# Loading the softmax divisors into 128 partitions: eight row broadcasts against one load with a repeated dimension

## The chip, the core and the metric

The kernel runs on one core of a Trainium2 chip. Its engines are TensorE (PE, matrix products), VectorE (DVE), ScalarE (ACT), GpSimd (POOL) and SyncE (SP), which here only issues transfers. SP's transfers run on the core's 16 DMA engines. The metric is the device time of one execution in microseconds, lower is better. Times shown are medians of runs of the same program.

## The reference

The reference is a gated cross-attention block followed by a mixture-of-experts block, over x of 4 batches x 1024 rows x 256. Cut to what matters here:

```
kh, vh = heads(ctx @ Wk.T), heads(ctx @ Wv.T)       # 154 keys, 16 heads of 16
qh     = heads(layernorm(x) @ Wq.T) / 4             # 1024 queries
scores = qh . kh + relative bias, causal mask
attn   = softmax(scores)                            # divides by the sum over the keys
x      = x + tanh(g_xattn) * (attn @ vh) @ Wo.T
x      = x + tanh(g_ffn)   * moe(layernorm(x))      # 8 routed experts, top 4, and a shared one
```

The change concerns the division in the softmax: the kernel first forms the products with the unnormalised exponentials, together with their sum over the keys, and then multiplies the products by the reciprocal of that sum.

## The kernel before

**Units.** The attention part works in eight units, numbered u = 2b + h: batch b of four, half h of its 1024 queries (512 queries). On every engine a unit is the function `unit(b, h, carry, ahead)`, with 20 steps `i` on PE, DVE and ACT. Step by step, PE computes the scores of the unit (`sT`, L917 to L924), ACT takes their exponential (`ex`, L503), PE multiplies by the values (`oT`, L938 and L942) and ACT copies the result to `raw` or `raw_first` (L493). Each engine does other work between: for the unit that follows, PE forms the scores again only to find each row's maximum (`smax`, L877), DVE reduces them (`mx`, L604), and PE, ACT and DVE project queries and keys of a later unit (`work`; L811, L822, L853; `ql` on DVE, L572). The maxima go through PE and DVE into `mt` (L659), and a transfer repeats them into `qs` (`qs<-mt`, L278), without which the next unit's scores can't start.

**Divisors.** The sums of a unit stand in four partitions of `raw`. They are divided one unit later. `divisors(u, h)` on SP is a chain of transfers, each of which waits for the one before it: `den_d<-raw` (L286) stores the 4 rows of 2048 sums in DRAM, `dent<-den_d` (L288) brings them back in 128 partitions x 64, DVE takes the reciprocal (L665), `rden_d<-dent` (L292) stores them in DRAM as 4 rows of 2048, and `at<-rden_d` (L296) brings them into the 128 partitions of `at`, in each of which 1024 numbers (4 KB) are wanted. Partition 32 j + 16 k + i needs the half k of row j, the same for all 16 values of i. Four short transfers (L290) shift part of `raw` between. `divide` on DVE (L671) then multiplies in two pieces, at steps 13 and 14 where h = 0 and at 12 and 13 where h = 1. PE projects `at` by `wo` (L953) at the end of the unit, or, for the last two units, in the expert part.

**The order around it.** All orders are written out by hand: each engine's program is a fixed list, and semaphores hold it back. In program order SP issues, after the `at` load: in units with h = 1 the keys of the next batch (`ks<-km`, L271), then queries; in units 2 and 4 (h = 0) only queries (`qs<-qh`, L267), which wait for `ql` of DVE. In unit 6, the last with h = 0, the weights of the expert part follow at once (L1127 and L1129, `cst`, `bias`, `gw` and nine pieces of `wx`), and behind them `qs<-mt`. On DVE, behind the first piece of `divide` in units 2 and 4, stand `ql` and further maxima. In the h = 1 units POOL subtracts the maxima from a whole score tile (L408) at the time at which DVE divides.

The divisors of units 0 to 5 are thus loaded and used in units 1 to 6, those of unit 6 in unit 7 and the first steps of the expert part, those of unit 7 in the expert part. There are eight `divisors` in all.

Of the kernel before, what the change touches and what calls it, by code (L numbers as in the profile page):

```python
# [23 lines left out]
H, HD = 16, 16  # L24
# [4 lines left out]
HALF = 512  # L29
# [53 lines left out]
def attention(nc, outer, ctx, x1, tg, t):  # L83
# [13 lines left out]
    def sb(name, shape, dt=F32, where=ctx):  # L97
        return where.enter_context(nc.sbuf_tensor(name, shape, dt))

    def sem(name):  # L100
        return outer.enter_context(nc.semaphore(name))
# [10 lines left out]
    at = sb("at", [P, 2, HALF], where=outer)  # L112
# [38 lines left out]
    rden_d = nc.dram_tensor("rden_d", (4, NG * HALF), F32).ap()  # L151
# [27 lines left out]
    shift_in, den_out, den_in, rden_s, rden_out, rden_in = sem("shift_in"), sem("den_out"), sem("den_in"), sem("rden"), sem("rden_out"), sem("rden_in")  # L179
# [44 lines left out]
    def batches(eng, unit):  # L224
        body(unit, 0, first=True)
        with eng.Fori(0, B - 2) as k:
            body(unit, k + 1)
        body(unit, B - 1, last=True)
# [18 lines left out]
    def sync(sp, load_weights):  # L247
        for dst, src in ((cst[:], t["cst"][:, 0:NKEPT]), (raw[:, 1, 0:2 * P], t["cst"][:, NKEPT:NKEPT + 2 * P])):
            sp.dma_start(dst, src).then_inc(w_in, 16)
        sp.dma_start(x1[:, 0:TU, :], t["x"][0][:, 0:TU, :]).then_inc(x_first, 16)  # L250
        for dst, src in ((raw[:, 0, :], t["wq"].rearrange("p c d -> p (c d)")), (rel[:], t["rel"]), (gates[:], t["gates"])):
            sp.dma_start(dst, src).then_inc(w_in, 16)
        sp.dma_start(ctxb[:], t["ctx"][0]).then_inc(c_in, 16)
        sp.dma_start(wk[:], t["wk"]).then_inc(kv_in, 16)
        sp.dma_start(wv[:], t["wv"]).then_inc(kv_in, 16)
        sp.dma_start(x1[:, TU:NT, :], t["x"][0][:, TU:NT, :]).then_inc(x_in[0], 16)
        sp.dma_start(wo[:], t["wo"]).then_inc(kv_in, 16)
        sp.wait_ge(kv_in, 3 * 16)
        for i in range(1, B):
            sp.dma_start(x1[:, i * NT:(i + 1) * NT, :], t["x"][i]).then_inc(x_in[i], 16)  # L260

        def q_stack(h, part):

            n = slice(h * HALF, (h + 1) * HALF)
            for r, src in enumerate((qh, ql, qh)):
                for i in (2 * part, 2 * part + 1):
                    sp.dma_start(qs[32 * r:32 * r + 32, i::4, n].bitcast(F32),  # L267
                                 src[32 * i:32 * i + 32, :, :].bitcast(F32)).then_inc(qs_in[h][part], 16)

        def k_stack(g):  # L270
            sp.dma_start(ks[0:96, 2 * g:2 * g + 2, :].bitcast(F32), km[:, 2 * g:2 * g + 2, 0:PAIR].bitcast(F32))\  # L271
                .then_inc(ks_in[g], 16)

        def m_stack(b, h):

            q0 = HALF // 2 if h == 0 else 0
            sp.wait_ge(mT_s, 2 * b + h + 1)
            sp.dma_start(qs[96:128, :, h * HALF + q0:(h + 1) * HALF].bitcast(F32),  # L278
                         mt[:, q0:HALF].unsqueeze(1).broadcast_to([32, NSTK, HALF - q0]).bitcast(F32)).then_inc(ms_in, 16)

        def divisors(u, h):

            kept = raws[h]

            sp.wait_ge(raw_s, NG * (u + 1))
            sp.dma_start(den_d.rearrange("j (g n) -> j g n", g=NG), kept[HD::32, :, :]).then_inc(den_out, 16)  # L286
            sp.wait_ge(den_out, 16 * (u + 1))
            sp.dma_start(dent[:], den_d.rearrange("j (p n) -> (j p) n", p=32)).then_inc(den_in, 16)  # L288
            for j in range(4):
                sp.dma_start(kept[32 * j + HD:32 * j + 32, 0:2, :], kept[32 * j:32 * j + HD, 2:4, :]).then_inc(shift_in, 16)  # L290
            sp.wait_ge(rden_s, u + 1)
            sp.dma_start(rden_d.rearrange("j (p n) -> (j p) n", p=32), dent[:]).then_inc(rden_out, 16)  # L292
            sp.wait_ge(rden_out, 16 * (u + 1))
            for j in range(4):
                for k in range(2):
                    sp.dma_start(at[32 * j + HD * k:32 * j + HD * (k + 1), :, :].rearrange("p g n -> p (g n)"),  # L296
                                 rden_d[j:j + 1, 2 * k * HALF:2 * (k + 1) * HALF].broadcast_to([HD, 2 * HALF]))\
                        .then_inc(rden_in, 16)

        def unit(b, h, carry, ahead):  # L300
            u = 2 * b + h
            if h == 0 and ahead:
                sp.wait_ge(v_ps, b + 1)
                sp.nop().then_inc(waited, 1)
                sp.dma_start(ctxb[:], t["ctx"][b + 1]).then_inc(c_in, 16)
            if carry and (h == 0 or ahead):
                sp.wait_ge(st_ps, NI * u)
                q_stack(1 - h, 1)
            if carry:
                divisors(u - 1, 1 - h)  # L310
            if h == 1 and ahead:
                sp.wait_ge(kl_s, 2 * (b + 2))
                sp.nop().then_inc(waited, 1)
                for g in range(NG - 1):
                    sp.wait_ge(st_ps, NI * u + 5 * (g + 1))
                    k_stack(g)
            if ahead:
                sp.wait_ge(work_free, NW0 + NWORK * b + Q_USE[h] + 2)
                sp.nop().then_inc(waited, 1)
                sp.wait_ge(st_ps, NI * u + 15)  # L320
                q_stack(h, 0)
            if h == 0 and not ahead:
                for part in range(2):
                    sp.wait_ge(qs_in[1][part], 16 * 6 * B)
                load_weights()
            if h == 0:
                m_stack(b, 1)
            elif ahead:
                m_stack(b + 1, 0)
                sp.wait_ge(st_ps, NI * (u + 1))  # L330
                k_stack(NG - 1)

        sp.wait_ge(work_free, 4)
        for part in range(2):
            q_stack(0, part)
        sp.wait_ge(kl_s, 2)
        for g in range(NG):
            k_stack(g)
        sp.wait_ge(work_free, 12)
        for part in range(2):  # L340
            q_stack(1, part)
        m_stack(0, 0)
        batches(sp, unit)
        divisors(2 * B - 1, 1)

    def gpsimd(pool):
# [192 lines left out]
    def vector(dve):  # L539
# [125 lines left out]
            nc.vector.reciprocal(dent[:], dent[:]).then_inc(rden_s, 1)  # L665

        def divide(u, h, groups=range(2)):
            dve.wait_ge(rden_in, 128 * (u + 1))
            dve.wait_ge(shift_in, 64 * (u + 1))
            for g in groups:  # L670
                nc.vector.tensor_tensor(at[:, g, :], raws[h][:, g, :], at[:, g, :], ALU.mult).then_inc(at_s, 1)  # L671
# [14 lines left out]
        def unit(b, h, carry, ahead):  # L686
# [3 lines left out]
            for i in range(NI):  # L690
# [16 lines left out]
                if i in DIVIDE[h] and carry and (h == 0 or ahead):  # L707
                    divide(u - 1, 1 - h, (DIVIDE[h].index(i),))
# [73 lines left out]
        def second_half():  # L782
            unused(Y_USE[0], B, 0)
            for pr in range(2):
                residual(B - 1, 1, pr, NW0 + Y_USE[0] + pr)

        return lambda: divide(2 * B - 2, 0), first_half, lambda: divide(2 * B - 1, 1), second_half

    def tensor(pe):
# [768 lines left out]
```

## Time and profile before

| | |
|---|---|
| median of 3 runs | 726.85 us (726.72 to 727.78) |
| the profiled execution | 730.77 us |
| its span, first to last instruction | 728.7 us |
| PE busy | 619.2 us, 85% of the span |
| DVE busy | 458.8 us, 63% |
| ACT busy | 276.1 us, 38% |
| POOL busy | 178.3 us, 24% |
| packets of SP's queue q1 | 39824, 58.25 MB, 28.9% of 16 DMA engines' span |
| mean granted TensorE clock | 0.938 |

The profiled execution took 730.77 us, of which 728.7 us lie between the first and the last instruction; all times of rows are within this span. A row of the timeline gives the start, the duration, the engine, the line of the kernel and what is written from what; "x8" means eight of one kind in a row, and a bracket tells how long the engine had stood idle and who ended that. "SPq" rows are transfers being issued: their duration is the time to issue, not to land. A row "DMA" in the chain of waits is a transfer in flight, from the start of its issue to its landing.

### The profile page before, as it was taken

The page shows a single profiled execution, that of the slowest core. Times are in us where ns is not written, and L with a number is a line of the kernel's source. Part 1 is how long each engine was busy: PE and PEld are TensorE (multiplying, and loading weights), DVE is VectorE, ACT ScalarE, POOL GpSimd, SP SyncE. Part 2 cuts the span into 40 slices and gives each one's busy share as a digit, 9 for nine tenths or more (in the row PEclk, how much of TensorE's full clock was granted, in tenths as well). Part 3 has the DMA queues.
Part 4 walks back from the last instruction along what each step waited for, and adds up shares of the span by engine and source line. Part 5 has one row for each costly group of instructions (what it writes and reads, how often), then busy time and mean ns, then how long its engine had stood idle before and what let it go on. Part 6 is the DMA issues. An engine that isn't in the chain of part 4 may idle for free.

```text
span 728.7 us, 10636 instructions
## 1 busy us (share of the span) xinstructions
PE 619.2 (85%) x3384; PEld 485.6 (67%) x3384; DVE 458.8 (63%) x884; ACT 276.1 (38%) x501; POOL 178.3 (24%) x177
## 2 busy tenths in 40 slices
PE   2665968788978987878667999999999999999997
PEld 2544745566645755554345888888888887888886
DVE  3677657868587758761277575756657475765653
ACT  2432456334733455344351422333242332324222
POOL 2151005300341007100111232232324223232222
PEclk9976989999989999999869999999999999999999
DMA  6850233524252333473212022031212202121220
GB/s 223 210 133 23 45 73 88 124 46 98 60 130 62 74 86 88 106 231 74 47 31 86 32 66 81 2 102 43 87 58 73 72 8 94 43 87 59 74 73 29
DMA packets 39856, 58.65 MB, mean 80 GB/s; under 512 B 7984, under 2 KB 21040, under 8 KB 39792
## 3 DMA queue, kind: packets, MB, share of 16 engines
q1 hardware_dynamic: 39824, 58.25, 28.9%
q8 instruction: 17, 0.28, 0.2%
q14 instruction: 15, 0.12, 0.0%
HBM read 31.76 MB, written 4.85 MB: 50 GB/s over the span
## 4 chain that ended last, share of the span: by engine, by line
issue 49%; PE 21%; DVE 11%; POOL 8%; DMA 5%; ACT 3%; SPq 2%; DVEq 0%; POOLq 0%; ACTq 0%
POOL hl L1172 4%; PE oT L938 3%; PE smax L877 3%; PE sT L918 3%; PE oT L942 3%; DMA qs<-mt 3%; DVE mx L604 2%; PE work L822 2%; SPq L296 2%; POOL d L399 2%; DVE mx L632 1%; PE sT L917 1%; DMA at<-rden_d 1%; PE work L853 1%; PE work L811 1%
## 5 line engine op out<-in xcount | busy, mean ns | idle before, releaser
L1172 POOL TENSOR_TENSOR hl<-sg,hh 128x512 fp32r<-128x512 f32 x72 | 93.2, 1296 | 249.6 <-ACT hh L1215 249.6
L503 ACT ACTIVATE ex<-sT 128x512 f32<-128x512 f32 (+1 forms) x160 | 91.9, 593 | 156.2 <-PE sT L918 130.7
L1209 ACT ACTIVATE sg<-pg 128x512 f32<-128x512 f32 x72 | 43.1, 598 | 199.2 <-PE pu L1455 198.4
L877 PE MATMUL smax<-km,qs 96*128 96x308 f32 (+1 forms) x244 | 86.9, 393 | 26.3 <-DVE mx L604 19.0
L604 DVE TENSOR_REDUCE mx<-smax 128x2 f32<-128x308 f32 x185 | 81.0, 472 | 35.8 <-PE smax L877 34.8
L877 PEld LDWEIGHTS smax<-km,qs 96*128 96x128 f32 x244 | 48.7, 209 | 60.5 <-DVE mx L604 35.4
L1470 PE MATMUL py<-wxl,hh 128*128 128x256 f32 x288 | 81.9, 284 | 4.2 <-DVE x L1353 3.1
L1470 PE MATMUL py<-wxh,hl 128*128 128x256 f32 x288 | 80.8, 281 | 0.0
L1470 PE MATMUL py<-wxh,hh 128*128 128x256 f32 x288 | 80.6, 280 | 0.0
L1341 DVE TENSOR_TENSOR sg<-cwb,sg 128x512 f32<-128x512 f32 x64 | 66.6, 1040 | 10.8 <-DMA cwb<-cwt_d 7.9
L1336 DVE TENSOR_TENSOR sg<-pu,sg 128x512 f32<-128x512 f32 x72 | 49.2, 684 | 28.4 <-ACT sg L1209 26.9
L918 PE MATMUL sT<-qs,ks 128*128 128x256 f32 (+1 forms) x128 | 53.4, 434 | 13.0 <-DMA qs<-mt 11.7
L1455 PE MATMUL pg<-x2l,wxh 128*128 128x512 f32 x144 | 60.3, 419 | 4.1 <-issue 4.1
L1470 PEld LDWEIGHTS py<-wxl,hh 128*128 128x128 f32 x288 | 54.3, 188 | 10.2 <-DVE x L1353 5.4
L1455 PE MATMUL pu<-x2l,wxh 128*128 128x512 f32 x144 | 57.9, 402 | 0.0
L1455 PE MATMUL pu<-x2h,wxl 128*128 128x512 f32 x144 | 57.8, 401 | 0.0
L1455 PE MATMUL pg<-x2h,wxh 128*128 128x512 f32 x144 | 57.6, 400 | 0.0
L1455 PE MATMUL pg<-x2h,wxl 128*128 128x512 f32 x144 | 57.5, 399 | 0.0
L1455 PE MATMUL pu<-x2h,wxh 128*128 128x512 f32 x144 | 57.3, 398 | 0.0
L1470 PEld LDWEIGHTS py<-wxh,hl 128*128 128x128 f32 x288 | 54.2, 188 | 2.7
L1470 PEld LDWEIGHTS py<-wxh,hh 128*128 128x128 f32 x288 | 54.6, 190 | 0.0
L1215 ACT CAST hh<-sg 128x512 fp32r<-128x512 f32 x72 | 44.0, 611 | 9.6 <-DVE sg L1341 9.3
(154 smaller groups left out, 1125.8 us busy)
## 6 DMA issues: line engine op xcount, KB each, us to landing
cwb<-cwt_d SPq DMA_DIRECT2D x64, 256.0 KB, 3.3
qs<-qh SPq DMA_DIRECT2D x64, 128.0 KB, 2.5
qs<-ql SPq DMA_DIRECT2D x32, 128.0 KB, 2.5
at<-rden_d SPq DMA_DIRECT2D x64, 64.0 KB, 2.2
out<-x SPq DMA_DIRECT2D x8, 512.0 KB, 4.3
ks<-km SPq DMA_DIRECT2D x16, 231.0 KB, 3.4
wx<-in_wx SPq DMA_DIRECT2D x9, 384.0 KB, 6.2
x<-in_x SPq DMA_DIRECT2D x3, 1024.0 KB, 8.6
```

The lines of the kernel that those rows point to most:

```text
L503: nc.scalar.activation(ex[:, g % 2, i % 5, q0:HALF], ST[i % 2][:, q0:HALF], ACT.Exp).then_inc(exp_s, 1)
L604: nc.vector.reduce_max(mx[:, m_tile(h, p), 2 * stk:2 * stk + 2], banks[q % len(banks)][:, 0:PAIR].rearrange("p (j k) -> p j k", j=2), AX_X)\
L877: last_one = nc.tensor.matmul(bank[:, 0:width], qs[0:96, s, tile * P:(tile + 1) * P], km[:, s, 0:width], start=True, stop=True)
L918: last_one = nc.tensor.matmul(out[:, q0:HALF], ks[:, s, j * KL:j * KL + P], qs[:, s, q], start=True, stop=True)
L938: nc.tensor.matmul(OT[32 * j:32 * j + 32, :], va[:, 4 * g + j, :], ex[:, g % 2, j, :], start=True, stop=True)
L1172: nc.gpsimd.tensor_tensor(hl[:, i % R, :], sg[:, i % R, :], hh[:, i % R, :], ALU.subtract).then_inc(hl_done, 1)
L1209: nc.scalar.activation(sg[:, i % R, :], PG[i % RG][:], ACT.Silu).then_inc(sg_s, 1)
L1215: nc.scalar.copy(hh[:, i % R, :], sg[:, i % R, :]).then_inc(hh_s, 1)
L1336: done = nc.vector.tensor_tensor(sg[:, i % R, :], PU[i % RG][:], sg[:, i % R, :], ALU.mult)
L1341: nc.vector.tensor_tensor(sg[:, i % R, :], cwb[:, e % RC, :], sg[:, i % R, :], ALU.mult)\
L1455: last = nc.tensor.matmul(out_[:], wa[:, e, w], xa[:, u, c, :], start=first, stop=(c == C - 1 and wa is wxh and xa is xh))
L1470: last = nc.tensor.matmul(y, ha[:, i % R, q], wa[:, e, 2 * C * I:XW], start=(e == 0 and s == 0 and j % 2 == 0), stop=(e == NE1 - 1 and s = ...
```

## The change

```diff
@@ divisors, on SP
-            for j in range(4):
-                for k in range(2):
-                    sp.dma_start(at[32 * j + HD * k:32 * j + HD * (k + 1), :, :].rearrange("p g n -> p (g n)"),
-                                 rden_d[j:j + 1, 2 * k * HALF:2 * (k + 1) * HALF].broadcast_to([HD, 2 * HALF]))\
-                        .then_inc(rden_in, 16)
+            sp.dma_start(at[:].rearrange("p g n -> p (g n)"),
+                         rden_d.rearrange("j (k n) -> j k n", k=2).unsqueeze(2).broadcast_to([4, 2, HD, 2 * HALF]))\
+                .then_inc(rden_in, 16)
@@ divide, on DVE
-            dve.wait_ge(rden_in, 128 * (u + 1))
+            dve.wait_ge(rden_in, 16 * (u + 1))
```

The eight loads of a unit, each of 16 partitions x 4 KB from one half row, become one load of 128 partitions x 4 KB. Its destination is the 128 partitions; its source is 8 half rows (j and k, which lie one behind the other in DRAM and so make one dimension of 8 with a step of 1024), then 16 repeats with a step of 0, then 1024 numbers. The same 512 KB are moved to the same places. The eight loads stand one behind the other in SP's program, so seven issues go in each of the eight units. DVE waits for one transfer's 16 instead of eight transfers' 128. No other instruction changes on any engine.

SP's program from the last of unit 5's transfers into unit 7, before. `at<-rden_d 16x1024 x8` is the group of eight:

```order
L267 DMA qs<-qh 32x2x512 x2
L286 DMA den_d<-raw 4x2048
L288 DMA dent<-den_d 128x64
L290 DMA raw<-raw 16x1024 x4
L292 DMA rden_d<-dent 128x64
L296 DMA at<-rden_d 16x1024 x8
L1127 DMA cst<-in_cst 128x583
L1127 DMA bias<-in_bias 128x8
L1127 DMA gw<-in_gw 128x16
L1129 DMA wx<-in_wx 128x768 x9
L278 DMA qs<-mt 32x8x512
```

The same place now (the lines behind the edit have moved up by two):

```order
L267 DMA qs<-qh 32x2x512 x2
L286 DMA den_d<-raw 4x2048
L288 DMA dent<-den_d 128x64
L290 DMA raw<-raw 16x1024 x4
L292 DMA rden_d<-dent 128x64
L294 DMA at<-rden_d 128x1x1024
L1125 DMA cst<-in_cst 128x583
L1125 DMA bias<-in_bias 128x8
L1125 DMA gw<-in_gw 128x16
L1127 DMA wx<-in_wx 128x768 x9
L278 DMA qs<-mt 32x8x512
```

One issue stands where eight stood, and the weights follow it directly. In the h = 1 units the keys follow it in the same way:

```order
L292 DMA rden_d<-dent 128x64
L294 DMA at<-rden_d 128x1x1024
L310 ISA
L313 REGISTER_ALU
L271 DMA ks<-km 96x2x308
```

Nothing has moved past anything else.

## Rows read from the trace of the kernel before

**Rows 1.** Page, last parts: DMA issues, KB each, median us to landing.
```profile
cwb<-cwt_d SPq DMA_DIRECT2D x64, 256.0 KB, 3.3
...
at<-rden_d SPq DMA_DIRECT2D x64, 64.0 KB, 2.2
```

**Rows 2.** Timeline of SP, units 1, 2, 4, 6 and behind.
```profile
117.93 3.58 SPq L296 DMA_DIRECT2D at<-rden_d  x8
...
159.89 3.58 SPq L296 DMA_DIRECT2D at<-rden_d  x8
166.83 1.32 SPq L267 DMA_DIRECT2D qs<-qh  x2
...
239.36 3.58 SPq L296 DMA_DIRECT2D at<-rden_d  x8
...
312.93 3.57 SPq L296 DMA_DIRECT2D at<-rden_d  x8
316.61 0.36 SPq L1127 DMA_DIRECT2D cst<-in_cst  x1
...
368.11 3.57 SPq L296 DMA_DIRECT2D at<-rden_d  x8
```

**Rows 3.** Chain of waits, units 2, 4 and 6: start, us, what.
```profile
163.05 2.17 DMA at<-rden_d
...
242.52 2.30 DMA at<-rden_d
256.49 4.53 DMA qs<-mt
...
316.08 2.34 DMA at<-rden_d
327.75 5.00 DMA qs<-mt
```

**Rows 4.** Timeline of DVE, units 1, 2, 4, 6 and the expert part.
```profile
123.83 4.36 DVE L671 TENSOR_TENSOR at<-raw_first,at 128x512 f32<-128x512 f32 x2
...
165.34 0.69 DVE L671 TENSOR_TENSOR at<-raw,at 128x512 f32<-128x512 f32 x1
...
244.34 0.48 DVE L604 TENSOR_REDUCE mx<-smax 128x2 f32<-128x308 f32 x1 [0.32 <-PE smax L877]
244.93 0.69 DVE L671 TENSOR_TENSOR at<-raw,at 128x512 f32<-128x512 f32 x1
...
318.45 0.69 DVE L671 TENSOR_TENSOR at<-raw,at 128x512 f32<-128x512 f32 x1 [3.25 <-DMA at<-rden_d]
...
382.71 1.29 DVE L671 TENSOR_TENSOR at<-raw,at 128x512 f32<-128x512 f32 x2
```

**Rows 5.** Timeline of POOL, unit 1.
```profile
123.39 3.61 POOL L408 TENSOR_TENSOR sx<-sx,mx 128x2048 f32<-128x2048 f32 x1 [4.73 <-DVE mx L622]
```

**Rows 6.** Timeline of PE, units 2 and 4, behind DVE's division.
```profile
166.69 0.76 PE L822 MATMUL work<-ctxb,wk 128*96 128x154 f32 x4 [0.16 <-DVE ql L572]
...
246.28 0.76 PE L822 MATMUL work<-ctxb,wk 128*96 128x154 f32 x4 [0.29 <-DVE ql L572]
```

**Rows 7.** Busy times in windows: PE, PEld, DVE, ACT, POOL, PEclk, DMA share, GB/s.
```profile
306.00:312.90 6.90, 6.90 (x49) 4.45 (x49) 5.54 (x15) 3.99 (x8) 0.00 (x0) 1.00 0.31 56
312.90:318.50 5.60, 2.89 (x20) 2.39 (x19) 2.18 (x6) 2.67 (x5) 0.00 (x0) 1.00 0.43 127
```

**Rows 8.** DMA, 346 to 352 us: eight loads at<-rden_d alone.
```profile
DMA packets 256, 0.52 MB, mean 87 GB/s; under 512 B 128, under 2 KB 128, under 8 KB 256
...
q1 hardware_dynamic: 256, 0.52, 33.2%
```

**Rows 9.** DMA, 354.9 to 357 us: one store den_d<-raw alone.
```profile
DMA packets 8, 0.03 MB, mean 16 GB/s; under 512 B 4, under 2 KB 4, under 8 KB 4
...
q1 hardware_dynamic: 8, 0.03, 6.6%
```

**Rows 10.** DMA, 386.2 to 387.6 us: one store cwt_d<-rows, 8 rows of 2 KB.
```profile
DMA packets 17, 0.03 MB, mean 23 GB/s; under 512 B 8, under 2 KB 8, under 8 KB 16
```

**Rows 11.** DMA, 327.5 to 333 us, GB/s in 40 slices: wx, then qs<-mt.
```profile
GB/s 425 402 402 447 447 380 380 447 358 246 224 216 305 290 209 246 156 209 246 223 223 149 223 179 223 238 238 179 149 194 45 60 30 15 15 0 0 0 0 0
```

## The prediction

> **What bounds the kernel now.** I read the page first. The loads of the divisors are small and many (64 of 64 KB, 2.2 us each to landing [rows 1]), so the question is where anyone waits for them. The timeline of SP says when they are issued: first issue to last issue 3.16 us, the group 3.58 us [rows 2]. The chain of waits gives the landing of the last: in unit 2 at 163.05 + 2.17 = 165.22, in unit 4 at 242.52 + 2.30 = 244.82, in unit 6 at 316.08 + 2.34 = 318.42 [rows 3]. From the first issue that is 5.33, 5.46 and 5.49 us. The timeline of DVE shows what this meets [rows 4]. The first division of unit 2 starts at 165.34 and that of unit 4 at 244.93, each about 0.1 us behind the landing. That of unit 6 starts at 318.45 after 3.25 us of idle time, ended by this very transfer. PE can't run on without DVE: it is busy for all 6.90 us ahead of 312.9, but for 2.89 of the 5.60 us until 318.5 [rows 7]. So unit 6 is a true stall, and units 2 and 4 stand at its edge. There PE waits already for `ql`, which DVE does right behind the division (0.16 and 0.29 us [rows 6]): a division that is late by a microsecond holds PE by about a microsecond.
>
> Elsewhere it is hidden. In unit 1 DVE divides from 123.83, but its two divisions take 4.36 us instead of two times 0.69, since POOL's subtraction runs from 123.39 to 127.00 beside them [rows 4, 5]. A load that lands by about 127, over 9 us after its first issue at 117.93 [rows 2], costs nothing. Units 3 and 5 repeat this. The last one is issued at 368.11 and used at 382.71 [rows 2, 4], which is 14.6 us of room.
>
> **The change, part by part.** SP loses seven issues in each of eight units, about 3.0 us of its time each. In units 2 and 4 SP's next issue is at 166.83 and waits for `ql` [rows 2], so this is worth nothing. In the h = 1 units the keys go out 3 us sooner and are wanted a unit later: nothing. In unit 6 the weights go out from 313.5 instead of 316.61. They are wanted far later, but `qs<-mt`, on which the next unit hangs, took 5.00 us there against 4.53 us in unit 4 [rows 3], because the weights were still streaming at 380 to 447 GB/s when it was issued [rows 11]. Sooner weights give back up to 0.5 us of this; I take 0.4.
>
> The other side is when the one load lands, L us after its issue. The size of the packets and their number stay: 128 of 4 KB. What changes is how many DMA engines they are dealt to. A transfer leaves one small completion packet for each engine it used: the eight present loads leave 128 small ones beside their 128 of data, so 16 engines each [rows 8]; the store of 4 rows leaves 4 beside 4 [rows 9]; the store of 8 rows leaves 8 beside 8 of data [rows 10], with one instruction fetch. The engines used follow the outermost dimension. The new load has 128 partitions outermost at its destination, but 8 half rows outermost at its source. I take 8 engines, with 16 packets each in a row.
>
> The Trainium skill states it outright (DMA: Bandwidth & Descriptors, Queues, rings and completion order and the section behind it, on why a DMA increments its semaphore by 16): the engine count is the largest number up to 16 that divides the slowest dimension of both sides. By that rule it is 8 here; the 4 and 8 completion packets agree. The same page's rules for kernel authors say to coalesce many small transfers into one, which speaks for the change and by itself would only bring the landing forward.
>
> How long is one packet on its engine? Eight loads keep 16 engines busy for 33.2% of 6.0 us: 0.332 x 6.0 x 16 / 128 = 0.249 us for 4 KB [rows 8]. The 8 KB packets of the 4-engine store took 0.066 x 2.1 x 16 / 4 = 0.554 us, or 0.277 us for 4 KB [rows 9]. The weights at 425 to 447 GB/s over 16 engines give 27 GB/s each, 0.15 us for 4 KB [rows 11]. Today's 64 KB load, with one packet on each engine, lands in 2.2 us [rows 1], so L = 2.2 + 15 packets + about 0.15 us for an issue with one dimension more. By the three prices L = 4.6, 6.1 and 6.5 us. The nearest rows are those of this very load and of a transfer on few engines, 0.25 and 0.28; between them L = 6.3. It replaces 5.33 to 5.49.
>
> The sum at L = 6.3: unit 2, landing at 159.89 + 6.3 = 166.19 against a start at 165.34, +0.85. Unit 4, 239.36 + 6.3 = 245.66 against 244.93, +0.75. Unit 6, 312.93 + 6.3 = 319.23 against 318.42, +0.8; there the weights now run beside it, up to 16 engines' worth, where before they came behind it: +0.4 by estimate (0 if the load keeps its place ahead of them, 1 if half its packets take a third longer). `qs<-mt` gives back 0.4. Units 1, 3, 5 and 7 are 0. Together +2.4 us: 730.77 becomes 733.2 for an execution like the profiled one, which stood 3.9 us above the median of the runs, and 726.85 becomes 729.2. The profiled one is one execution with the recording on; I apply the difference to the median.
>
> **Rivals.**
>
> Fewer engines, but fast ones. If the eight engines stream as they do for the weights, L is 4.6 to 5.6. Units 2 and 4 gain nothing, since DVE comes to the division from a maximum that ends at 244.82 in unit 4, 0.1 us before the division starts now [rows 4], and lose nothing. Unit 6 gains up to 0.9 and pays 0.4 for the weights, `qs<-mt` gives 0.4: from -0.9 to +0.5, so 726.0 to 727.4. For it: 0.15 us is what an engine can do. Against it: `cwb`, a broadcast from DRAM on all partitions with 8 packets of 2 KB for each engine if it uses 16, lands in 3.3 us [rows 1]; that is 1.1 us over the 64 KB load for 7 packets more, 0.16 us for only 2 KB.
>
> All 16 engines. If the destination's 128 partitions decide, each engine has 8 packets: L = 2.2 + 7 x 0.25 + 0.15 = 4.1 us. Unit 6's stall of 3.25 us shrinks by 1.4, the load is done before the weights come in force, `qs<-mt` gives 0.5: -1.9 to -2.1, 724.9 us, faster. This is the case on the other side, and it decides from the count of engines alone: the small packets of a unit would be 16. For it: the destination has 128 outermost, and no row here has a transfer whose two sides differ in this. Against it: both stores with few rows.
>
> A fourth one, that nothing at all changes because SP's time was free, is the first rival's middle.
>
> **How the numbers follow.** Chances: forecast 0.38 (728.2 to 730.3); fast engines 0.31 (725.7 to 728.2); 16 engines 0.14 (724.2 to 725.7); crowded partitions 0.17 (730.3 to 732.5). What a measurement can tell from no change is 0.2%, 1.45 us: faster is below 725.4, slower above 728.3. Faster: 0.8 of the 16-engine case and little of the fast one, 0.13. Slower: the forecast nearly whole and the crowded case, 0.5. The rest, 0.37, is the same. The likeliest case is at 729.2. The range 725.0 to 731.4 leaves out most of the 16-engine case and the upper half of the crowded one.
>
> **What would show it.** In the changed profile a window with one `at<-rden_d` alone would have 128 data packets and 8 small ones; 16 would refute the forecast. The issue list would give its landing: 6.3 us right, under 5.6 wrong. DVE's idle time ahead of the first division would be about 0.9 us in units 2 and 4 and about 4.4 in unit 6, `qs<-mt` in unit 6 about 4.6 us, and the divisions in units 1, 3 and 5 still about 4 us for two. If the landing is late but units 2 and 4 show no stall on PE, the term of the sum for them is wrong; if the landing is at 4 us and the time falls, the count of engines is.

## The result and the profile after

The changed kernel takes 733.45 us (median of 7 runs, 730.67 to 736.86) against 726.85 us (7 runs, 725.13 to 728.97). The ratio is 1.009, with a 95% interval from 1.0059 to 1.0122: slower, by 4.3 to 8.9 us. Measured a second time beside other runs of the kernel before (e9 below), the ratio was 1.006 (1.0034 to 1.0086), 2.5 to 6.3 us. The forecast was slower, 729.2 us; the first time lies beyond the range that went with it, 725.0 to 731.4. Here and below a ratio is estimated from all runs of both kernels, so it isn't quite the quotient of the two medians, and the microseconds beside an interval are the ratio's.

First, what the new load is. A window with one such load alone, in unit 7 of the changed kernel:

```profile
DMA packets 136, 0.52 MB, mean 62 GB/s; under 512 B 8, under 2 KB 8, under 8 KB 136
...
q1 hardware_dynamic: 136, 0.52, 23.6%
```

128 packets of data and 8 small ones: 8 engines, 16 packets each. Before, the same 128 packets of data came with 128 small ones [rows 8]. The engines' time is 0.236 x 8.4 x 16 / 128 = 0.248 us for each 4 KB, the 0.249 of before.

The chain of waits of the changed kernel (start, us, what) shows what that does to the landing, in units 1, 2, 4 and 6:

```profile
120.39 8.14 DMA at<-rden_d
162.28 6.66 DMA at<-rden_d
...
244.29 6.65 DMA at<-rden_d
...
318.88 8.32 DMA at<-rden_d
337.04 4.31 DMA qs<-mt
```

Against 5.33 to 5.49 us from first issue to last landing [rows 2, 3], it is 6.65 us in units 2 and 4, where nothing runs beside it, and over 8 us in units 1 and 6. The timeline of SP says what stands beside it there:

```profile
120.39 0.67 SPq L294 DMA_DIRECT2D at<-rden_d  x1
121.18 4.52 SPq L271 DMA_DIRECT2D ks<-km  x3
...
318.88 0.65 SPq L294 DMA_DIRECT2D at<-rden_d  x1
319.64 0.39 SPq L1125 DMA_DIRECT2D cst<-in_cst  x1
320.07 0.43 SPq L1125 DMA_DIRECT2D bias<-in_bias  x1
320.54 0.55 SPq L1125 DMA_DIRECT2D gw<-in_gw  x1
321.13 5.15 SPq L1127 DMA_DIRECT2D wx<-in_wx  x9
```

One issue takes 0.65 us. Then the keys follow in unit 1, the weights in unit 6. Both used to be issued behind the eighth load: in unit 6 at 316.61 [rows 2], when the last load had 1.8 us left to its landing at 318.42 [rows 3]. On DVE the divisions of units 1, 2, 4 and 6 answer to [rows 4]:

```profile
128.56 2.09 DVE L669 TENSOR_TENSOR at<-raw_first,at 128x512 f32<-128x512 f32 x2 [2.19 <-DMA at<-rden_d]
169.06 0.69 DVE L669 TENSOR_TENSOR at<-raw,at 128x512 f32<-128x512 f32 x1 [1.33 <-DMA at<-rden_d]
...
251.05 0.69 DVE L669 TENSOR_TENSOR at<-raw,at 128x512 f32<-128x512 f32 x1 [1.32 <-DMA at<-rden_d]
...
327.23 0.69 DVE L669 TENSOR_TENSOR at<-raw,at 128x512 f32<-128x512 f32 x1 [6.00 <-DMA at<-rden_d]
```

Units 2 and 4 now wait 1.3 us, unit 6 waits 6.00 instead of 3.25. Unit 1 also waits, 2.19 us, and yet its two divisions end at 130.65, 10.26 us after the first issue; before it was 123.83 + 4.36 - 117.93 = 10.26 us [rows 2, 4]. POOL's subtraction explains it:

```profile
125.85 3.61 POOL L406 TENSOR_TENSOR sx<-sx,mx 128x2048 f32<-128x2048 f32 x1 [4.73 <-DVE mx L620]
```

It ends at 129.46 here and at 127.00 before [rows 5], and both times DVE's two divisions end 1.19 us behind it. The late load only shortened the time that they run beside it. On PE, unit 2 (compare [rows 6]) and the stall of unit 6 (compare [rows 7]):

```profile
170.41 0.76 PE L820 MATMUL work<-ctxb,wk 128*96 128x154 f32 x4 [1.50 <-DVE ql L570]
```
```profile
320.70:327.20 6.50, 1.12 (x10) 0.89 (x8) 0.48 (x1) 1.47 (x3) 0.00 (x0) 0.91 0.93 182
```

From the issue of one `qs<-mt` to the next is one unit. The table has the profiled executions of all kernels with the single load in a unit, and of those with the eight loads there. Kernels with another form of the load are left out, and in unit 6 those with the weights moved (e3, e7):

| | eight loads, us | one load, us | difference of the means |
|---|---|---|---|
| unit 1 | 39.22 38.80 39.00 38.81 | 39.06 39.42 39.87 38.81 | +0.3 |
| unit 2 | 41.68 40.67 42.18 42.03 | 43.03 43.46 42.02 43.50 | +1.4 |
| unit 3 | 37.56 37.24 38.86 38.74 | 38.89 37.10 37.50 38.16 | -0.2 |
| unit 4 | 41.95 42.69 41.64 41.72 | 43.01 43.16 43.14 43.41 | +1.2 |
| unit 5 | 39.00 38.83 37.59 37.59 | 38.91 37.58 39.13 37.39 | 0.0 |
| unit 6, weights right behind the load | 32.26 32.00 | 35.52 35.47 35.36 35.78 | +3.4 |

Part of unit 6's loss is given back behind it. From its `qs<-mt` to the last store of sums (`den_d<-raw`, unit 7) it took 27.15 and 26.85 us with eight loads, 24.95 three times and once 26.47 with one. Of these 2 us, `qs<-mt` itself is 0.4 to 0.7: 5.00 and 4.75 us with eight loads (e1), 4.31 to 4.34 with one. The rest goes with the granted clock. Five microseconds of unit 7, at the same distance behind `qs<-mt`, in the kernel before and in the changed one (PE, PEld, DVE, ACT, POOL, PEclk, DMA share, GB/s):

```profile
333.00:338.00 5.00, 5.00 (x17) 2.28 (x17) 0.00 (x0) 2.18 (x5) 0.00 (x0) 0.66 0.01 3
```
```profile
342.30:347.30 5.00, 4.49 (x25) 1.54 (x17) 0.00 (x0) 3.99 (x8) 0.00 (x0) 1.00 0.01 3
```

PE stood idle for `qs<-mt` in both. Before, its clock was partly at 1.2 GHz behind that wait (0.66 on the mean) and it did 17 matmuls; in the changed kernel it was at 2.4 GHz and it did 25 in less time. The five microseconds behind unit 6's division show the opposite. They are, in this order, of the kernel before, of the changed one, and of e7, which has the eight loads:

```profile
318.45:323.45 5.00, 3.87 (x18) 2.04 (x19) 3.70 (x8) 0.60 (x1) 0.00 (x0) 0.69 0.94 297
```
```profile
327.23:332.23 5.00, 3.87 (x15) 1.92 (x16) 3.22 (x7) 0.60 (x1) 0.00 (x0) 0.50 1.04 399
```
```profile
318.74:323.74 5.00, 3.86 (x15) 1.92 (x16) 3.22 (x7) 0.60 (x1) 0.00 (x0) 0.57 0.00 0
```

With eight loads and the weights moved, e7 has a unit 6 of 33.72 us and 25.07 us behind it. So a longer unit 6 with a shorter stretch behind it also comes without the single load (e4 and e8, with sixteen engines, have 24.9 and 25.0 us there too); what sets the clock in these two places stays open. The two together are steadier: 59.4, 58.9 and 58.8 us with eight loads (before, e1, e7), 60.5, 60.4, 60.7 and 61.8 with one (changed, e2, e9, e5). The means differ by 1.8 us, and that is the price of unit 6, as near as the profiles tell.

Such spells of the low clock fall here and there from execution to execution: the first profiled execution of the changed kernel was 2.5 us behind before any load of the divisors was issued (`qs<-mt` of unit 1 at 98.62 against 96.08 us). One profile against one profile would therefore mislead; the means of the table's rows do so less.

### The profile page after: what moved, and what is told of

It reads as the page before. It is cut to its first block, busy times and chain, and to the rows that moved or that the text cites. A ratio compares the mean times of both kernels' runs of the same rounds, so it can differ in the third digit from the quotient of the medians.

```text
span 734.5 us, 10576 instructions
## 1 busy us (share of the span) xinstructions
PE 619.8 (84%) x3384; PEld 486.1 (66%) x3384; DVE 452.9 (62%) x884; ACT 276.3 (38%) x501; POOL 178.0 (24%) x177
## 4 chain that ended last, share of the span: by engine, by line
issue 47%; PE 22%; DMA 10%; DVE 10%; POOL 7%; ACT 2%; DVEq 0%; POOLq 0%; SPq 0%; ACTq 0%
DMA at<-rden_d 6%; POOL hl L1170 4%; PE oT L936 4%; PE smax L875 3%; PE sT L916 3%; PE oT L940 3%; DMA qs<-mt 2%; DVE mx L602 2%; PE work L820 2%; DVE mx L630 1%; PE sT L915 1%; PE work L809 1%; DMA rden_d<-dent 1%; PE work L851 1%; PE work L951 1%
## 5 line engine op out<-in xcount | busy, mean ns | idle before, releaser
L1453 PE MATMUL pg<-x2l,wxh 128*128 128x512 f32 x144 | 60.4, 419 | 4.1 <-issue 4.1
```

The source lines that it names most:

```text
L1453: last = nc.tensor.matmul(out_[:], wa[:, e, w], xa[:, u, c, :], start=first, stop=(c == C - 1 and wa is wxh and xa is xh))
```

## The experiments

**t1, the load's form by itself.** Behind the last store of the kernel before, forms of the load with nothing beside them, each waited for, all twice:

```diff
+        for _ in range(2):
+            alone((full, changed))                               # 8 rows, each x 16: the change
+            alone(*[... for r in range(8)])                      # the eight loads
+            alone((full, flat[:, 0:N]))                          # 128 different rows of in_wx
+            alone((full, rows[0:1].broadcast_to([P, N])))        # one row x 128
+            alone((full, own16))                                 # 16 rows, each x 8
+            alone((full, <8 rows of in_wx, 27 KB apart, x 16>))
+            alone(*[... for j in range(4)])                      # 4 loads of 32 partitions, 2 rows each
+            alone((wx[0:32, 0:4, 0:768], <8 rows x 16>))         # 32 partitions, 4 pieces of 3 KB
+            alone((wx[:, 0, 0:768], <8 rows x 16>))              # 128 partitions, 3 KB
```

> The kernel before, with transfers added behind its last store that have nothing beside them, each form waited for before the next, all twice. They write over buffers that are no longer needed; the computation is whole. My theory: the engine count follows the source's outermost dimension, and an engine needs about 0.25 us for each 4 KB packet of this load, so the one load of the change (128 data packets, 8 small) takes 6.6 us from issue to landing, the eight loads 5.4, one load from 128 different rows or from 16 rows repeated 8 times (16 small packets) under 4.5. If it is the number of engines alone that counts, 8 engines on 32 partitions (4 x 3 KB each) take as long as 8 engines on 128 partitions (3 KB each), about 5.2 us. If crowded partitions count (engines whose partitions lie 32 apart share a way into memory), the 32-partition form, whose engines are on 8 different groups of four partitions, is faster by a third or more: 3.5 to 4 us. If the rereading of the same DRAM row is what costs, the form with one single row on 128 partitions is the slowest of the 16-engine forms and the load with 8 rows far apart is as slow as that with 8 adjacent rows. Four loads of 32 partitions (source outermost 2, so 2 engines each, the same two): 64 packets on each of two engines, 12 to 18 us; a rival without the rule of the source's outermost dimension has them at about 5.

SP's timeline; from one start to the next is the time of one form. First round:

```profile
725.66 0.69 SPq L1163 DMA_DIRECT2D at<-rden_d  x1
732.45 3.85 SPq L1163 DMA_DIRECT2D at<-rden_d  x8
737.98 0.36 SPq L1163 DMA_DIRECT2D at<-in_wx  x1
741.55 0.34 SPq L1163 DMA_DIRECT2D at<-rden_d  x1
745.17 0.62 SPq L1163 DMA_DIRECT2D at<-in_wx  x1
749.93 0.63 SPq L1163 DMA_DIRECT2D at<-in_wx  x1
756.62 2.58 SPq L1163 DMA_DIRECT2D at<-rden_d  x4
769.41 0.71 SPq L1163 DMA_DIRECT2D wx<-rden_d  x1
773.70 0.59 SPq L1163 DMA_DIRECT2D wx<-rden_d  x1
779.13 0.59 SPq L1163 DMA_DIRECT2D at<-rden_d  x1
```

The form of the change takes 6.79 us (6.67 in the second round), eight loads 5.53 (5.49). 128 different rows take 3.57 and one row on 128 partitions 3.62 (3.32), on 16 engines; so reading a DRAM row again costs nothing visible. 16 rows, each on 8 partitions, take 4.76 (4.60). Eight rows far apart take 6.69 (5.94), so neighbouring rows are not what makes the form slow. The four loads of two rows each take 12.79 (12.69). Their window, and those of the last two forms:

```profile
DMA packets 136, 0.52 MB, mean 40 GB/s; under 512 B 8, under 2 KB 8, under 8 KB 136
...
q1 hardware_dynamic: 136, 0.52, 10.3%
```
```profile
q1 hardware_dynamic: 136, 0.39, 22.7%
```
```profile
q1 hardware_dynamic: 136, 0.39, 28.4%
```

Four loads leave 8 small packets, two each: two engines, as expected. A packet of 4 KB takes them 0.103 x 13.0 x 16 / 128 = 0.167 us, not the 0.25 of eight engines. And eight engines with the same bytes in the same number of packets are done in 4.29 us on 32 partitions (four partitions to an engine; 0.227 x 5.0 x 16 / 128 = 0.142 us for 3 KB), in 5.43 us on 128 (0.178 us). So two things are slow in the changed form: half the engines, and how these eight lie on the partitions. The second is less than was expected: the form on 32 partitions was to be faster by a third or more, 3.5 to 4 us, and is faster by a fifth. The form with 16 rows was expected under 4.5 us and took a little more. In kind the second is the crowded-partitions rival, whose price of 6.8 to 7.1 us was closer than the forecast's 6.3. Why the layout costs is not shown. That partitions 32 apart share a way, as the Trainium skill has it (SBUF — State Buffer, Door 1: The DMA port swizzle), was not tried with other distances. And it doesn't explain one row: in the kernel before, 16 engines write 16 neighbouring partitions at once and take the same 0.249 us for 4 KB [rows 8].

**e1 and e2, where it costs.** The single load where the units hide it, and where they don't:

```diff
+            if h == 0:                    # e1; in e2: h == 1
+                sp.dma_start(at[:]..., rden_d...broadcast_to([4, 2, HD, 2 * HALF])).then_inc(rden_in, 16)
+            else:
+                <the eight loads>
```

> One load where the divisors are those of an even unit (issued in units 1, 3, 5, 7), the eight loads elsewhere. My theory: the load lands 8 us after its issue there, since the keys' transfers run beside it, but DVE's two divisions would wait for POOL anyway and end at the same time; 726.9 us, within 1 us of before. Rival (every late landing costs, about 1 us in each of units 1, 3 and 5): 729 to 730.

> One load where the divisors are those of an odd unit (issued in units 2, 4, 6 and once in the expert part), the eight loads elsewhere. My theory: here lies the whole loss, +1.3 and +1.1 us in units 2 and 4 and +3 in unit 6: 732 to 733.5 us, as the changed kernel. Rival (all units alike): half the loss, 730. In unit 6 the division on DVE waits 6.0 us for the load.

e1: 728.16 us against 728.36, ratio 0.9997 (0.9974 to 1.0021), though its load landed as late as in the changed kernel and DVE waited 2.16 us for it in unit 1:

```profile
118.53 8.10 DMA at<-rden_d
```
```profile
126.65 2.12 DVE L676 TENSOR_TENSOR at<-raw_first,at 128x512 f32<-128x512 f32 x2 [2.16 <-DMA at<-rden_d]
```

e2: 732.99 us, ratio 1.0057 (1.0028 to 1.0086), +4.2 us (2.0 to 6.3), with 5.94 us of waiting in unit 6. It has the single load once more in the expert part, where DVE shows no wait ahead of the division. Within the noise the whole loss is in units 2, 4 and 6. A wait that DVE shows is not yet a loss: in e1 it took the place of another.

**e3, the weights out of the way.**

```diff
-                load_weights()
             if h == 0:
                 m_stack(b, 1)
+                if not ahead:
+                    load_weights()
```

> The changed kernel with the expert part's weights issued behind qs<-mt in unit 6 instead of ahead of it. My theory: the weights, 3 us sooner now, run beside the one load on the same engines and cost it 1.7 us; without them it lands 6.65 us after its issue, DVE waits 4.4 us instead of 6.0, and the time is 731.5 to 732, 1.5 us below the changed kernel. Rival (the load in unit 6 is slow for a reason of its own): it stays at 8.3 us and the time with it. The weights are used from about 355 us and arrive by 350: no loss there.

Unit 6 in the chain and on DVE:

```profile
314.74 6.68 DMA at<-rden_d
331.62 4.41 DMA qs<-mt
```
```profile
321.44 0.69 DVE L670 TENSOR_TENSOR at<-raw,at 128x512 f32<-128x512 f32 x1 [4.36 <-DMA at<-rden_d]
```

The load is back at 6.68 us. The ratio is 1.0039 (1.001 to 1.0067), +2.8 us. This says that the weights beside it cost the load 1.6 us. That the time gains the same is not shown, since the intervals of e3 and of the changed kernel overlap.

**e4 and e8, sixteen engines.** The sums are stored twice, `dent` is 128 x 128, and the load has 16 rows, each repeated 8 times. e8 has the late weights too.

```diff
+            for c in range(2):
+                sp.dma_start(den_d[:, :, c, :], kept[HD::32, :, :].rearrange("j (k g) n -> j k (g n)", k=2))\
+                    .then_inc(den_out, 16)
...
+            sp.dma_start(at[:].rearrange("p g n -> p (g n)"),
+                         rden_d.unsqueeze(1).broadcast_to([16, HD // 2, 2 * HALF])).then_inc(rden_in, 16)
```

> One load again, but from 16 DRAM rows instead of 8, each repeated 8 times: the sums are stored twice in DRAM, so that the divisors' reciprocals (128 x 128 now) leave 16 rows of 1024. My theory: the load's speed hangs on the number of engines and on how their partitions lie; with 16 engines it lands 4.7 us after its issue where nothing is beside it (as the same form did alone), against 5.4 for eight loads and 6.7 for the changed one. Then no unit is later than before: units 2 and 4 as before, unit 6's wait of DVE 2.5 to 3.3 us. Time 726.5 to 728.5 beside a before of 728, the same as before. Rival (a single load is slow whatever its engines, since DVE must wait for all 512 KB at once): as the changed kernel, +5 us.

> Both changes that helped together: one load from 16 rows (16 engines) and the expert part's weights behind qs<-mt. My theory: in unit 6 the load lands 4.7 to 4.9 us after its issue, with nothing beside it, instead of 5.7; DVE waits 2.7 to 3.1 us, below the 3.25 us of the kernel before; qs<-mt 4.4 us. That is 1.0 to 1.5 us below the sixteen-engine kernel alone and 2 to 3 us (0.3 to 0.4%) below the kernel before: faster than both. Rival (the sixteen-engine kernel was only lucky with the clock): within 1 us of before.

Units 3 and 6 of e4, then unit 6 of e8, in the chain:

```profile
198.49 4.90 DMA at<-rden_d
...
311.70 5.71 DMA at<-rden_d
```
```profile
313.34 4.72 DMA at<-rden_d
```

A single load it is, and the loss is gone: e4 726.48 us against 728.45, ratio 0.9982 (0.9961 to 1.0004); e8 0.9991 (0.9972 to 1.0009). Against the changed kernel both are faster (the interval of e9, 1.0034 to 1.0086, lies above both), against the kernel before neither is. DVE's wait in unit 6 was 3.92 us in e4 and 2.91 in e8, a third of a microsecond better than before. The load alone gains 0.8 us against eight loads (4.72 to 5.49); the chain of transfers ahead of it, 7.7 us from `den_d<-raw` to the load's issue instead of 7.3, costs about half of that, and in e4 the weights cost another microsecond (5.71). The 2 to 3 us that e8 was to gain over the kernel before did not come: its interval reaches from -2.0 to +0.7 us. e4 changes the number of engines and the layout together, so the kernel's own runs don't tell the two apart; only t1 does, at eight engines.

**e5, unit 6 alone.** The single load in unit 6, eight elsewhere.

```diff
+            if isinstance(u, int) and u == 2 * B - 3:
+                <the single load>
```

> The kernel before with the one load in unit 6 alone, where the weights follow. My theory: unit 6 becomes 3.2 us longer (load 8.3 us, DVE waits 6.0 us), and unit 7 gives back up to 2.2 us where TensorE's granted clock keeps at its high level behind qs<-mt as in the profiles of the changed kernel: +1 to +3 us. Rival (units 2 and 4 carry the loss): no change. If unit 7 starts at the low clock as before, +3.

730.31 us against 728.45, ratio 1.003 (1.0006 to 1.0054), +2.2 us (0.4 to 3.9); the load took 8.41 us. So about half of the loss of 4.4 us is this one unit (1.8 us by the profiles above).

**e6, a stronger dose.** Four loads of two rows each, in all units.

```diff
-            for j in range(4):
-                for k in range(2):
+            for j in range(4):
+                sp.dma_start(at[32 * j:32 * j + 32, :, :]..., <rows 2 j and 2 j + 1>...broadcast_to([2, HD, 2 * HALF]))
```

> Four loads of 32 partitions each from two rows in all units: by my theory two engines carry all 128 packets, 12.7 us to landing, as alone. Units 2 and 4 lose 7.3 us each and unit 6 at least 7.3 and up to 9; in units 1, 3 and 5 the cover ends 10.3 us after the issue, so they now lose 2.4 us or more each: +29 to +34 us in all. Rival (no cover in units 1, 3, 5, all cost what they are late): +45. Rival (the engines are not set by the source's rows): under +5.

776.19 us against 728.45, ratio 1.0649, +47 us: more than the 29 to 34 expected. In unit 1 the last of the four landed 14.2 us after the first issue (the keys beside it again). DVE's divisions ended 15.5 us after it, 5.3 later than the 10.26 of the cover, and the unit was 44.46 us long, 5.5 more than the mean of before. So the cover of 10.3 us holds. Unit 2 became 10.1 us longer than the mean of before, with a wait of 7.46 us on DVE; the clock is part of the difference. Unit 2 in windows, ahead of the wait, in it and behind it:

```profile
166.00:174.00 8.00, 8.00 (x53) 6.13 (x52) 5.41 (x12) 3.62 (x7) 0.00 (x0) 1.00 0.09 29
174.00:178.00 4.00, 0.91 (x7) 0.65 (x6) 0.00 (x0) 0.97 (x2) 0.00 (x0) 1.00 0.13 52
178.00:181.20 3.20, 0.00 (x0) 0.00 (x0) 0.00 (x0) 0.00 (x0) 0.00 (x0) 0.60 0.10 41
181.20:185.00 3.80, 2.45 (x10) 2.43 (x11) 2.83 (x6) 0.43 (x1) 0.00 (x0) 0.50 0.25 52
```

The granted clock fell while PE stood idle, and the work that came back at 181.2 ran at 1.2 GHz for 3.8 us. Behind the 1.3 us stalls of the changed kernel the granted clock stayed at 1.00, in unit 2 (169 to 185 us) as in unit 4 (251 to 267). In unit 6 of e6 the weights follow the loads:

```profile
370.06 0.69 DVE L670 TENSOR_TENSOR at<-raw,at 128x512 f32<-128x512 f32 x1 [14.87 <-DMA at<-rden_d]
```

The last of the four landed 17.2 us after the first issue there, and the unit was 46.35 us long, 14.2 more than the mean of before, where up to 9 was expected. So the expectation fell short in three places: the keys beside the loads in units 1, 3 and 5, the clock in units 2 and 4, and the weights in unit 6.

**e7, late weights in the kernel before.** The edit of e3.

> The kernel before with the expert part's weights issued behind qs<-mt in unit 6. My theory: qs<-mt takes 4.5 instead of 5.0 us, the load of the divisors is as before (5.4 to 5.5 us, since the weights came behind it anyway): -0.5 us, within noise. Rival (the weights disturbed nothing, or are now late for the expert part, which uses them from about 355 us): no change or up to +2 us. It tells how much of the gain of late weights in the changed kernel comes from the load and how much from qs<-mt.

727.76 us against 728.45, ratio 0.9991 (0.9967 to 1.0015): no difference. `qs<-mt` took 4.44 us instead of 5.00, and the load landed as before, 5.51 us after the first issue. So what late weights give in e3, if anything, is the load's. Unit 6 was nevertheless 33.72 us long, with DVE's division at the same place as before (22.98 us behind `qs<-mt`, before 22.96) and the lower clock behind it, as shown above.

**e9, the changed kernel again.**

> The changed kernel itself, beside the same runs of the kernel before. The kernel with the one load in units 2, 4 and 6 lost 4.2 us, that with it in units 1, 3, 5 and 7 nothing; if these are all, the changed kernel loses 4 to 4.5 us. If the first measurement (+6.6 us, with an interval from +4.3 to +8.9) holds, some 2 us come only with both together.

731.77 us against 727.84, ratio 1.006, +4.4 us (2.5 to 6.3). e1 and e2 account for it. Nothing beyond the noise is left that only both together would cost.

## Why the prediction was right in direction and too small

- **Eight engines by the source's outermost dimension.** Right: 8 small packets, and 2 for each of t1's four loads. The rule on the engine count in the Trainium skill (DMA: Bandwidth & Descriptors, Why a DMA increments its semaphore by 16 and not by 1) held where the two sides of a transfer differ, which no row of before showed. The advice in the Trainium skill to coalesce small transfers (the same page, Rules for kernel authors) did not hold here: eight transfers of 64 KB landed in 5.4 us and one of 512 KB in 6.65, since the one had half the engines.
- **L = 6.3 us.** Measured 6.65 alone. The packet's price of 0.25 us was right (0.248). What was short is the rest. The issue was put at 0.15 us more than before and took 0.65 against 0.42, and even so 2.2 + 15 x 0.248 + 0.23 is only 6.15: another 0.5 us is not resolved. Against the forecast's 6.3 this is 0.35 us in each of three units, 1.1 us in all.
- **The weights beside the load in unit 6, "+0.4 by estimate".** This is the term that failed. The load took 8.32 us there, 1.66 more than alone, and 6.68 with the weights moved (e3). Even the upper bound of 1 was too low, and by its own words (8 of 16 packets of 0.25 us, each a third longer) it would be 0.7. The estimate asked whether the load keeps its place ahead of the weights. It had nearly all of its 16 packets on each of eight engines still to write when the weights' transfers came, on all sixteen (they were issued from 0.76 us behind it); whether the two met on the engines or on the way to the partitions no run here tells.
- **Units 2 and 4, +0.85 and +0.75.** Measured +1.4 and +1.2. PE lost what DVE lost, about one for one, as argued from `ql` [rows 6]: DVE waited 1.33 and 1.32 us, and PE 1.50 in both, 1.34 and 1.21 more than before.
- **Units 1, 3, 5 and 7 at nothing.** Right (e1), by the cover that was named, POOL's subtraction, even with 8.1 us of landing, which the prediction did not have. The keys are what ran beside that load; no run moved them, so that they are the cause is argued, not shown.
- **`qs<-mt` gives back 0.4.** It gave 0.4 to 0.7 (5.00 and 4.75 to 4.31). With it, the stretch behind unit 6 became 2.0 us shorter in three of four profiles and 0.5 in one, at another granted clock; no step had that, nor the clock behind unit 6's division.
- **The sum.** Forecast +2.4. By the table's means it is +1.4, +1.2 and +3.4, less 1.7 behind unit 6: +4.3, beside the 4.4 of e9 and at the lower end of the first measurement's 4.3 to 8.9. The profiles thus agree with the second measurement; why the first was higher is not known. Of the 1.9 us that the forecast is short of this, about half is in units 2 and 4 and half in unit 6.
- **The range** reached 731.4 as the crowded-partitions case at its middle. That case was true in kind. The range held neither its upper half nor a larger price for the weights. With the ratio of e9 the time would be 731.2 us, just inside the range. That would not have made the forecast's terms right.

## What to carry to other kernels

Before joining transfers, look at the outermost dimension of both sides: it sets how many DMA engines work, and a source that repeats few rows cuts them. Count the small packets of a window with that transfer alone; they say how many engines it had. And ask what the freed queue will issue next: here it sent nine weight transfers of 384 KB after the very load that everyone waited for.

## What the runs showed of the hardware

- Eight engines that each write 16 partitions need 0.25 us for 4 KB (changed kernel), two such engines 0.167 us (t1); eight on 32 partitions need 0.142 us for 3 KB, on 128 partitions 0.178 us (t1).
- 512 KB on eight engines landed in 6.65 us alone and in 8.3 us with 384 KB transfers issued right behind it (e3 and the changed kernel); on sixteen engines it was 4.72 and 5.71 us (e8, e4).
- 512 KB to 128 partitions from one DRAM row land as fast (3.3 to 3.6 us) as from 128 rows (3.5 to 3.6 us).
- An issue with a repeated middle dimension holds SP for 0.56 to 0.71 us, a plain one for 0.33 to 0.42.
- In a stall of about 7 us the granted clock fell, and PE worked at the lower level for 3.8 us behind it (e6, unit 2); behind stalls of 1.3 us it stayed at 1.00 (changed kernel, units 2 and 4).
